# A first stage in four pipeline steps instead of three: a group's low half, router product and logits move to the next step

## The reference

```python
x = x + tanh(g_xattn[0]) * xattn0(layernorm(x), ctx, w_q, w_k, w_v)
x = x + tanh(g_ffn[0])   * moe0(layernorm(x), Wg, W1, b1, W2, b2)     # 8 experts, top 2
x = x + tanh(g_xattn[1]) * xattn1(layernorm(x), ctx, ctx, mask, ...)  # 16 heads
x = x + tanh(g_ffn[1])   * moe1(layernorm(x), ...)                    # 8 experts, top 2, and a shared one

def xattn0(x1, x2):            # one head of width 128
    q, k, v = x1 @ w_q.T, x2 @ w_k.T, x2 @ w_v.T
    return softmax(q @ k.T / sqrt(128)) @ v
def moe0(x):
    probs = softmax(x @ Wg)    # the router's logits: 8 per token
    ...                        # top 2, normalised; relu(x @ W1 + b1) @ W2 + b2 per expert
```

## Time and profile before

| | value |
|---|---|
| median of three runs | 736.52 us |
| profiled execution, device time | 737.57 us |
| its span, first to last instruction | 735.8 us |
| PE busy | 638.7 us, 87% |
| DVE busy | 556.7 us, 76% |
| ACT busy | 426.4 us, 58% |
| POOL busy | 103.7 us, 14% |
| mean granted TensorE clock | 0.917 of full speed |

### The profile page before, as it was taken

One profiled execution on the slowest core, in us unless ns is written; L12 is line 12 of the kernel. 1 busy time (PEld: TensorE's weight loads), 2 busy tenths in 40 slices (PEclk: granted clock), 3 DMA queues, 4 the chain that ended last, 5 costly groups with the idle time before them and its releaser, 6 DMA issues.

```text
span 735.8 us, 12635 instructions
## 1 busy us (share of the span) xinstructions
PE 638.7 (87%) x4078; PEld 498.4 (68%) x4078; DVE 556.7 (76%) x1275; ACT 426.4 (58%) x665; POOL 103.7 (14%) x131
## 2 busy tenths in 40 slices
PE   5766665799999999998599999999997399999996
PEld 3654443587787787777377777767775277888884
DVE  2676656698898898888467878787776688888885
ACT  3433221487777777776267777777775155555553
POOL 3444331020000000000400221122022100000000
PEclk9867665799999999999889999999999599999998
DMA  5313100000000000001242334233400000010000
GB/s 161 110 55 107 35 9 0 1 0 1 1 0 0 0 0 0 0 17 56 52 126 80 79 97 121 79 81 91 115 1 1 1 0 1 15 29 14 14 15 29
DMA packets 23704, 29.33 MB, mean 40 GB/s; under 512 B 3313, under 2 KB 17522, under 8 KB 23666
## 3 DMA queue, kind: packets, MB, share of 16 engines
q1 hardware_dynamic: 23666, 28.84, 13.7%
HBM read 19.99 MB, written 8.85 MB: 39 GB/s over the span
## 4 chain that ended last, share of the span: by engine, by line
PE 66%; DVE 20%; issue 5%; ACT 4%; POOL 2%; DMA 1%; DVEq 1%; SPq 0%; ACTq 0%; POOLq 0%
PE psum L397 12%; PE psum L398 12%; PE psum L399 12%; PE psum L1247 5%; PE psum L1262 3%; DVE c_mx L1418 3%; PE psum L1237 2%; DVE c_sm L1424 2%; DVE xn L326 2%; PE psum L1238 2%; PE psum L386 2%; PE psum L914 2%; PE psum L1568 2%; DVE stats L294 1%; PE psum L345 1%
## 5 line engine op out<-in xcount | busy, mean ns | idle before, releaser
L397 PE MATMUL psum<-xh,w_hi 128*128 (+1 forms) x248 | 102.6, 414 | 2.6 <-DVE d_hr L1656 2.1
L1359 ACT ACTIVATE c_pt<-psum 77x512 f32<-77x512 f32 x128 | 74.8, 586 | 46.2 <-PE psum L1247 46.2
L398 PE MATMUL psum<-xl,w_hi 128*128 (+1 forms) x248 | 99.1, 400 | 0.0
L399 PE MATMUL psum<-xh,w_lo 128*128 (+1 forms) x248 | 98.8, 398 | 0.0
L980 ACT ACTIVATE b_hr<-psum,b1s 128x512 f32<-128x512 f32 x128 | 80.8, 685 | 15.6 <-PE psum L399 15.5
L864 DVE TENSOR_TENSOR b_hl<-b_hs,b_hh 128x1024 fp32r<-128x1024 f32 x64 | 78.2, 1221 | 15.4 <-ACT b_hh L858 15.3
L1040 DVE TENSOR_TENSOR b_hs<-b_hr,psum 128x1024 f32<-128x1024 f32 x64 | 77.8, 1215 | 14.6 <-ACT b_hr L980 13.1
L858 ACT ACTIVATE b_hh<-b_hs 128x1024 fp32r<-128x1024 f32 x64 | 67.9, 1061 | 33.2 <-PE psum L399 33.1
L1247 PE MATMUL psum<-ident,c_pf 128*77 128x128 f32 x512 | 74.8, 283 | 0.1
L1247 PEld LDWEIGHTS psum<-ident,c_pf 128*77 128x77 f32 x512 | 58.3, 149 | 14.6 <-issue 10.6
L1418 DVE TENSOR_REDUCE c_mx<-psum 128x8 f32<-128x616 f32 x64 | 50.9, 796 | 20.1 <-PE psum L1238 19.9
(11 more groups left out here) (209 smaller groups left out, 1246.2 us busy)
## 6 DMA issues: line engine op xcount, KB each, us to landing
w_hi<-c_q_spread SPq DMA_DIRECT2D x24, 256.0 KB
stage<-in_weights SPq DMA_DIRECT2D x8, 576.0 KB, 4.9
c_q_spread<-w_hi SPq DMA_DIRECT2D x7, 512.0 KB, 3.7
ctxg<-in_ctxT SPq DMA_DIRECT2D x16, 156.0 KB, 4.5
c_k_spread<-w_lo SPq DMA_DIRECT2D x8, 312.0 KB, 2.2
x_all<-in_x SPq DMA_DIRECT2D x8, 256.0 KB, 2.8
out_dram<-x_all SPq DMA_DIRECT2D x8, 256.0 KB, 2.3
c_kb<-c_k_spread SPq DMA_DIRECT2D x48, 39.0 KB
```

What stands on the lines that cost most here:

```text
L397: pe.matmul(o, wh, h, start=start, stop=False)
L398: pe.matmul(o, wh, l, start=False, stop=False)
L399: return pe.matmul(o, wl, h, start=False, stop=stop)
L1359: a_.activation(pt[:, q % NC4, :], bank[2 + q % 2][0:S2, :], ACT.Copy).then_inc(pt_done, 1)
```

## The change

`pool_a`, `pe_a`, `act_a` and `dve_a` go through `pipeline4`. What was done for `t` behind the transposes (low half, router product, copy of its transposed logits, transposes back, copy of the logits) is done for `u`, one step later, and early in that step: on DVE the low half is first and the logits copy stands between the softmax front of m and the statistics of a; on PE the product stands behind the scores, and the transposes back behind keys and values; on ACT the copy is the first item. PE gets one new wait: the transposes of t into bank 6 wait until the logits of u have been copied out of it. POOL's and SP's work is the same. All norms stay on DVE. The late set-up and the routing stand in step 10, with the last group as `u`.

```diff
@@ pool_a
-            def step(a, m, t):
+            def step(a, m, t, u):
 ...
-            pipeline(q, step)
+            pipeline4(q, step)
@@ pe_a
             # scores of m
+                if u:
+                    if u.i is None and u.c == 0:
+                        pe.wait_ge(s_split, 1)
+                    lg0.pe_product(pe, u)
+                    if not t:
+                        pe_setup_late(pe)
             # keys and values of a
+                if u:
+                    lg0.pe_transpose(pe, u)
             # transposes of m
                 if t:
+                    if u:
+                        pe.wait_ge(lg0.lg_copied, t.at(1, 0))
                     ln1.pe_transpose(pe, t)
             # output of m, transposes of a
-                if t:
-                    if t.i is None and t.c == 0:
-                        pe.wait_ge(s_split, 1)
-                    lg0.pe_product(pe, t)
-                    if not m:
-                        pe_setup_late(pe)
-                    lg0.pe_transpose(pe, t)
@@ act_a
+                if u:
+                    lg0.act_copy(a_, u)
+                    if not t:
+                        act_setup_late(a_)
+                        Route(0, HEAD, rt_tail).act_ratio(a_)
             # keys, values, exponential, probabilities, weights, high halves
-                if t:
-                    lg0.act_copy(a_, t)
-                    ...
@@ dve_a
+                if u:
+                    ln1.dve_low(v, u)
+                    if not t:
+                        route.second(v)
+                        dve_setup_late(v)
+                        route.weights(v)
+                        lg0.dve_copy(v, u)
             # residual and statistics of t, maximum and subtraction of m
+                if u and t:
+                    lg0.dve_copy(v, u)
             # statistics of a, norm of t, norm of a, sums of m
-                if t:
-                    ln1.dve_low(v, t)
-                    if not m:
-                        ...
-                    lg0.dve_copy(v, t)
```

More of the change, by code:

```diff
@@ L574, in step @@
                     ln0.pe_transpose(pe, a)
-                if t:
-                    if t.i is None and t.c == 0:
-                        pe.wait_ge(s_split, 1)
-                    lg0.pe_product(pe, t)
-                    if not m:
-                        pe_setup_late(pe)
-                    lg0.pe_transpose(pe, t)
-            pipeline(pe, step)
+            pipeline4(pe, step)
         pe_parts.append(pe_a)
         def act_a(a_):
-            def step(a, m, t):
+            def step(a, m, t, u):
+                if u:
[3 more added lines that the diff above has]
+                        Route(0, HEAD, rt_tail).act_ratio(a_)
                 if a:
@@ L605, in step @@
                     ln0.act_high(a_, a)
-                if t:
-                    lg0.act_copy(a_, t)
-                    if not m:
-                        act_setup_late(a_)
-                        Route(0, HEAD, rt_tail).act_ratio(a_)
-            pipeline(a_, step)
+            pipeline4(a_, step)
         act_parts.append(act_a)
@@ L659, in step @@
                     v.wait_ge(a_rg, m.at(1, 1))
-                if t:
-                    ln1.dve_low(v, t)
[L662 to L665, removed]
-                    lg0.dve_copy(v, t)
-            pipeline(v, step)
+            pipeline4(v, step)
         dve_parts.append(dve_a)
```

## The result

| | before | after |
|---|---|---|
| median | 737.0 us (4 runs) | 728.62 us (728.11 to 731.14, 4 runs) |
| ratio to before | | 0.9874, 95% interval 0.9853 to 0.9895 |
| span of the profiled run | 735.8 us | 726.1 us |
| mean granted clock | 0.917 | 0.924 |
| DVE's wait at the logits copy, five steps | 17.6 us (34 to 110 us) | 12.6 us (34 to 102 us) |

The medians are 8.4 us apart, and the ratio on record says 1.3%; the forecast was 726.4 us. All of it but 0.4 us is inside stage A: its last logits copy starts at 129.51 us instead of 138.84, 9.3 us earlier, and the spans of the profiled runs differ by 9.7. A ratio leaves out runs over 1.5% above the fastest of their kernel; in this document that is one, the profiled run with POOL's low half held back (722.14 us).

What follows compares the result with a forecast made beforehand. No engine fills a stage A step; a chain of waits bounds it. Gains of 2.0 (start), 4 x (15.28 - 14.65) (steps) and 5.7 (end) sum to 10.2 us: median forecast 726.4 us, range 723.5 to 729.

Steps and rivals of the forecast that it cites:

- The residual moves up: DVE, stage A: the residual of t follows the low half of u, starting at about N+1.9.
- The new wait at the logits copy: DVE, ready at N+5.2, stands 3.7 us for PE's transposes back at the low clock, behind keys and values.
- N: End of the norm of a in a step, from which times in the step are counted; 44.04 us in step 3 before.
- The contention: POOL's low half starts within 0.2 us of DVE's norm of a; 3.42 us charged for the norm every step.
- The clock: PE's full clock returns between N+5.7 and N+7.4; interval 14.4 to 14.9 us, 14.65 taken.
- Start of the stage: Stage A up to step 3: its norm of a ends at 42.0 instead of 44.04 us, a gain of 2.0.
- the end of the stage: Stage A, from N of step 7 to the last group's residual: 11.2 us instead of 16.92, a gain of 5.7.
- That PE stays at the low clock: First rival, one form: low clock through each step, intervals 15.5 to 15.95, 729.7 to 731.5 us; chance 0.15 for both forms.
- that POOL comes before the whole norm: First rival, other form: POOL's low half blocks all four norm instructions, about 3.8 us instead of 3.42; chance 0.15 shared.
- the low half slips past the norm: Second rival: POOL's low half hits L658 instead, or the clock stays up; interval 12.35 or 12.1, some 717 us; chance 0.15.
- The slow side: Third rival: the logits copy in DVE's queue delays every step; loses above an interval of 17.2, 738.1 us; chance 0.06.
- the end of the stage gains nothing: Fourth rival: steps balance out and the last group's chain starts when it did, 736.5 us; chance 0.04.

Runs made afterwards that it cites:

- PE kept busy: Changed kernel plus ten transposes of the identity, of no use to the result, on PE ahead of the transposes of a: 724.7 us, ratio 0.9832.
- both edits: Changed kernel with the logits copy behind the statistics of a and POOL's low half held back until L670: 701.95 us, ratio 0.9484.

## Why the prediction was right

**The residual moves up.** Right: 0.61 us from the start of the low half to that of the residual, where 0.9 was worked out; before 4.58.

**The new wait at the logits copy.** Right in kind and size: N+8.0 to N+8.5 were forecast for its end, and in steps 4 to 7 it ended at N+8.0, N+7.55 (N = 57.29, end 64.84), N+8.96 (the step at the low clock: N = 71.55, end 80.51) and N+8.0. The waits were 1.3 to 3.3 us, against the 3.7 forecast at the low clock and 2.8 to 3.3 with its return. Moving the copy by one place (710.28 us) and moving keys and values (713.07 us) both show it as a cost, though each removed contention as well. This wait is nearly all the clock's: the forecast's own figures for the full clock (DVE ready at N+5.2, the copy at N+5.6) leave 0.4 us of it, and with PE kept busy it was 0.3.

**The contention.** Right: the low half started within 0.2 us of the norm in all five steps, and the charge of 3.42 us met 3.33 to 3.41. Two steps with the clock up show the whole amount, 12.18 against 9.95 us. But the charge was for a norm that starts first, and in steps 4 to 7 POOL was first; that the two cost nearly the same was luck. The bound for "POOL first", 3.8 us, was 0.45 too high. The Trainium skill, "SBUF — State Buffer", section "SBUF: two separate sides", says that the loser blocks fully until the other's instruction ends. With POOL first by 0.14 us (68.08 against 68.22), the norm's first instruction ended 0.08 us behind POOL's, so its wait agrees. But only the other three, 0.77 us, came on top, where my reading of the rule had added all four.

**The clock.** Right in the mean, with the pattern of a return during the run from scores to values: three intervals of 14.3 to 14.5 and one of 15.46 against 14.65 forecast. The full clock came back at about N+6.2, 5.4, 8.1 and 6.4 in steps 4 to 7, where N+5.7 to N+7.4 was estimated; the late one is the long step. The estimate that the low clock alone gives 15.5 and the full one 12.1 was borne out by 15.46 (15.27 with PE kept busy) and 12.18.

**Start of the stage.** This term was mis-sized: 2.0 us were forecast, 1.25 came (N of step 3 at 42.79 instead of 44.04). I had let PE run at the full clock there. First, in step 2 POOL's low half now hit L670:

```profile
28.54 2.62 POOL L473 TENSOR_TENSOR w_lo<-stage,w_hi 128x1152 fp32r<-128x1152 f32 x1 [1.45 <-ACT w_hi L468]
...
28.95 2.24 DVE L670 TENSOR_SCALAR a_rg<-a_ri,tg 128x4 f32<-128x4 f32 x1
...
31.22 0.69 DVE L358 TENSOR_TENSOR xl<-psum,xh 128x512 fp32r<-128x512 f32 x1
...
32.06 0.77 PE L375 MATMUL psum<-xh,w_hi 128*128 128x512 f32 x1 [1.19 <-DVE xl L358]
```

The low half starts at 31.22 behind it and ends 0.4 us later than the 31.51 that I had taken. That alone was no delay against the forecast: the product starts at 32.06, where its leg had 32.40. But PE had idled 1.19 us before it, and the granted clock was 0.50 from there to about 35 us: L375 took 0.77 us, against 0.49 in step 2 of the kernel before. From the start of the product to the end of the transposes back (36.41) were 4.35 us, against 3.0 forecast. The logits were copied at 36.64 instead of 35.5; from the statistics to the norm it took 1.54 instead of 1.80, and the rest was as forecast. So the size that failed is that of PE's leg, which I had at the full clock. Two runs show what brought it down. With the low half held back L670 took 0.23 us, the product (L375, 0.48) followed the scores at once, and the same leg took 2.78 us at the full clock. With PE kept busy L670 was hit (2.13 us), but ten transposes had filled PE's time ahead of the transposes of a, and the leg again took 2.77. So the collision cost its time through PE's idle stretch and the clock. In step 2 of the kernel before, the norm of a had ended at 29.38 and L658 at 30.24, just ahead of POOL's start at 30.33.

**The other terms** stand: 4 x (15.28 - 14.68) = 2.4 forecast as 2.5, and the end of the stage from N of step 7 (101.52) to the last residual:

```profile
112.76 1.13 DVE L632 SCALAR_TENSOR_TENSOR x_all<-psum,a_rg,x_all 128x128 f32<-128x128 f32 x4 [0.32 <-PE psum L580]
```

That is 11.24 us against 11.2. Together 1.25 + 2.4 + 5.7 = 9.3, against 10.2 forecast and 9.7 between the spans. The eleventh step cost nothing, as argued: from the last residual to the last logits copy are 16.75 us before and after. The medians put the gain at 8.4 us (1.3% by the ratio), inside the range by a wide margin.

**The rivals.** That PE stays at the low clock was true of one step; that POOL comes before the whole norm was true of four, but cost 3.33 us and not 3.8. That the low half slips past the norm never happened here; the run that forced it had 712.75 us where I had put 717, with a spread that reaches to 722 where the clock went low. The slow side had its mechanism right (the copy in DVE's queue is a cost in each step), but its decision point of N+10.8 was never near. That the end of the stage gains nothing is refuted by its 5.7 us.

## What to carry to other kernels

When a wait is moved in a software pipeline, look at what stands behind it in its engine's order: here the copy left one stall for another, and moving it one place further, behind work that needs nothing from it, brought twice what the change did (a part of it by the contention that went with it). Look for two engines whose work excludes each other at the same point of every step, and hold back the one whose result is not due; a regular collision of 2.6 us took 2.2 us from every step here. And where PE has idle time, give each step's estimate at both clock levels: 12.2 and 15.3 us for the same work were found in one run.

## What was not expected of the hardware

The clock fell without any long idle time of PE. In steps 3 to 7 of the changed kernel PE idled at most 2.5 us at a stretch, and yet the clock was low from about the end of each step until the values of the next (in step 6 to their end). With both edits, at 9.16 us a step and 6.54 us of PE work, it stayed at 1.00 and PE never idled over 1.2 us; in the changed kernel's longest step, 15.46 us with 11.14 us of PE work (the same instructions, most of them slow), it stood at 0.61. A short step alone doesn't keep it up: with only the copy moved, steps of 9.61 and 10.43 us had 0.72 and 0.67, behind a blocked norm beside which PE had idled 2.6 to 2.7 us. What rule the clock follows is not shown.

With the low half held back alone, runs of one kernel spread from 710.55 to 722.14 us. The mean clocks don't order them (0.936 for 710.79 us, 0.922 for 717.68, but 0.928 for 722.14), and only one of these runs was looked at step by step, so the cause of the spread stays open.
